# Chunk 0 of a Mamba block between two feed-forward halves: B is turned behind the step-size matmuls

## What is computed

```python
x = x + 0.5 * ffn(layernorm(x), ...)
x = x + mamba(layernorm(x), ...)
x = x + 0.5 * ffn(layernorm(x), ...)
```

```python
proj = einsum('blh,oh->bol', x, W_in)          # h and gate, 1024 channels each
h = silu(causal_conv4(h) + conv_b)
ts, Bm, Cm = split(einsum('bil,oi->blo', h, Wx), [128, 144])
ts, Bm, Cm = rms(ts, dt_ln_w), rms(Bm, b_ln_w), rms(Cm, c_ln_w)
delta = softplus(einsum('blr,ir->bil', ts, Wdt) + dt_bias)
# over l: s = exp(delta * A) * s + delta * B * h ; y = sum_n s * C
y = (y + D * h) * silu(gate)
return einsum('bil,hi->blh', y, Wout)
```

## Time and profile before

| | |
|---|---|
| median of 3 runs | 2776.47 us (2773.37 to 2778.87) |
| the profiled execution | 2791.37 us |
| its span, first to last instruction | 2789.4 us |
| mean granted TensorE clock | 0.912 |
| busy share: TensorE, VectorE, ScalarE, GpSimd | 85%, 88%, 63%, 81% |

### The profile page before, as it was taken

How to read it: one execution, slowest core, us unless ns; L and a number is a source line. 1 busy time by engine, 2 the same in 40 slices (tenths; PEclk the granted TensorE clock), 3 DMA queues, 4 the chain that set the end, 5 groups by cost and what they waited for, 6 DMA issues and landing times. The chain is left out here.

```text
span 2789.4 us, 38187 instructions
## 1 busy us (share of the span) xinstructions
PE 2381.1 (85%) x12266; PEld 1961.2 (70%) x12266; DVE 2461.4 (88%) x3119; ACT 1758.2 (63%) x2995; POOL 2272.8 (81%) x1393
## 2 busy tenths in 40 slices
PE   7888887888688998889988998789987984699968
PEld 6766776676467886677767887677866863577747
DVE  5679997897899998999989999999999987999972
ACT  5585677575657665675568765666667756474531
POOL 2369689789977999699987989699996999888842
PEclk9898998899789999999989999999998996599979
DMA  8754835837575577846787578856788486366634
GB/s 289 261 196 150 299 114 174 303 118 270 175 251 198 165 243 263 295 148 224 235 294 246 157 231 281 304 166 190 237 264 280 122 307 242 106 219 203 231 95 137
DMA packets 293424, 605.61 MB, mean 217 GB/s; under 512 B 23008, under 2 KB 23776, under 8 KB 293216
## 3 DMA queue, kind: packets, MB, share of 16 engines
q1 hardware_dynamic: 293216, 603.08, 64.7%
HBM read 450.42 MB, written 152.57 MB: 216 GB/s over the span
## 5 line engine op out<-in xcount | busy, mean ns | idle before, releaser
L2053 POOL TENSOR_TENSOR sbuf<-dus,bring 128x1024 f32<-128x1024 f32 x512 | 1219.8, 2396 | 175.1 <-PE pt L1489 86.1
L1658 ACT ACTIVATE pa<-dls,cst 128x512 f32<-128x512 f32 x1024 | 699.2, 690 | 498.1 <-DVE sbuf L1840 484.7
L1489 PE MATMUL pt<-ident,sbuf 128*128 128x128 f32 x4096 | 660.7, 298 | 188.3 <-DVE sbuf L1840 68.9
L1489 PEld LDWEIGHTS pt<-ident,sbuf 128*128 128x128 f32 x4096 | 537.3, 154 | 318.2 <-DVE sbuf L1840 98.2
L1407 PE MATMUL pm<-xT,wring 128*128 128x512 f32 x2816 | 712.4, 401 | 17.7 <-DVE xT L1712 9.8
L1840 DVE TENSOR_TENSOR_SCAN sbuf<-pa,carry,sbuf 128x512 f32<-128x512 f32 x512 | 635.7, 1268 | 23.4 <-ACT pa L1658 13.6
L1840 DVE TENSOR_TENSOR_SCAN sbuf<-pa,sbuf 128x512 f32<-128x512 f32 x512 | 605.9, 1207 | 34.3 <-POOL sbuf L2053 19.8
L1851 DVE SCALAR_TENSOR_TENSOR acc<-pt,cT,acc 128x512 f32<-128x512 f32 x768 | 547.5, 737 | 81.3 <-PE pt L1489 71.9
L1420 PE MATMUL pm<-wring,act 128*128 128x512 f32 x2176 | 582.4, 410 | 26.9 <-DMA wring<-wsp 8.0
L1407 PEld LDWEIGHTS pm<-xT,wring 128*128 128x128 f32 x2816 | 519.2, 190 | 120.8 <-issue 17.2
L1420 PEld LDWEIGHTS pm<-wring,act 128*128 128x128 f32 x2176 | 401.7, 193 | 114.2 <-issue 12.0
(11 more groups left out here) (153 smaller groups left out, 2283.8 us busy)
## 6 DMA issues: line engine op xcount, KB each, us to landing
wring<-wsp SPq DMA_DIRECT2D x408, 512.0 KB, 4.3
bring<-b_d SPq DMA_DIRECT2D x256, 256.0 KB, 3.9
xn_d<-tb SPq DMA_DIRECT2D x24, 1024.0 KB, 9.7
xnb<-xn_d SPq DMA_DIRECT2D x19, 1024.0 KB, 7.8
x_d<-tb SPq DMA_DIRECT2D x16, 1024.0 KB, 5.3
sg_d<-hd SPq DMA_DIRECT2D x64, 256.0 KB, 4.5
tb<-x_d SPq DMA_DIRECT2D x16, 1024.0 KB, 7.2
spw<-u_d SPq DMA_DIRECT2D x30, 512.0 KB, 4.5
```

What stands on the lines that cost most here:

```text
L1489: ins = e.matmul(pt[u.pt[tt]][:, k * P:(k + 1) * P], sbuf[:, u.s3, k, tt * P:(tt + 1) * P], ident[:, :], is_transpose=True, start=True, st ...
L1658: e.activation(pa[k % 2][:, :], dls[:, k, :], ACT.Exp, scale=col(C_A + (4 * u.ig + k) * N + u.n)).then_inc(S.a_exp, 1)
L2053: e.tensor_tensor(sbuf[:, u.s3, h * m:(h + 1) * m, :], dus[:, h * m:(h + 1) * m, :], bring[:, u.s2:u.s2 + 1, :].broadcast_to([P, m, TC]), ...
```

## The change

The turn of B leaves the `dt0` unit and becomes a unit of its own, `turn_b`, with the same wait, transposition, copy and stores. For chunks 1 to 7 it is added right behind the turn of ts, as before. For chunk 0 it is added inside `softplus`, behind the `dt` units of the first two quarters and ahead of the softplus steps. So on TensorE and in ScalarE's main thread B's turn and its copy come behind the twelve step-size matmuls and the four copies of their banks. Banks are taken in that order too.

```diff
@@ dt0 @@
         u = self.add("m", Unit("dt0", c))
-        u.ts, u.bn = x.ts, x.bn
+        u.ts = x.ts
@@
         self.bank_free[u.bank] = self.tsT[c] = (u.hi, u.lo)
-        u.bank2, u.bank2_before = self.bank()
-        u.pe2 = self.up(S.p_bt)
-        self.free["bn"] = (u.pe2,)
-        u.bt_before = self.get("bT")
+        if c:
+            self.turn_b(c, x.bn)
+            self.softplus(c, 0)
+        else:
+            self.softplus(c, 0, 1)
+
+    def turn_b(self, c, bn):
+        S = self.S
+        u = self.add("m", Unit("turn_b", c))
+        u.bn = bn
+        u.bank, u.bank_before = self.bank()
+        u.pe = self.up(S.p_bt)
+        self.free["bn"] = (u.pe,)
+        u.before = self.get("bT")
         u.bt = self.up(S.a_bt)
-        self.bank_free[u.bank2] = (u.bt,)
+        self.bank_free[u.bank] = (u.bt,)
         u.kept = self.b_there[c] = self.up(S.st_b, 64)
         self.add("b_out", u)
         self.free["bT"] = (u.kept,)
-        if c:
-            self.softplus(c, 0)
-        else:
-            self.softplus(c, 0, 1)
 
     def softplus(self, c, *parts):
         made = [self.soft_start(c, part) for part in parts]
+        if c == 0 and 0 in parts:
+            self.turn_b(c, self.x_small[c].bn)
         for step in ("soft1", "soft2", "soft3"):
@@ pe_main @@
-                        q.wait_ge(u.bn, *u.bank2_before)
-                        e.matmul(pm[u.bank2][:, 0:P], bn[:, :, :].rearrange("p a b -> p (a b)"), ident[:, :],
+                    elif u.kind == "turn_b":
+                        q.wait_ge(u.bn, *u.bank_before)
+                        e.matmul(pm[u.bank][:, 0:P], bn[:, :, :].rearrange("p a b -> p (a b)"), ident[:, :],
                                  is_transpose=True, start=True, stop=True).then_inc(S.p_bt, 1)
@@ act_main @@
-                        q.wait_ge(u.pe2, *u.bt_before)
-                        e.activation(bT[:, :], pm[u.bank2][:, 0:P], ACT.Copy).then_inc(S.a_bt, 1)
+                    elif u.kind == "turn_b":
+                        q.wait_ge(u.pe, *u.before)
+                        e.activation(bT[:, :], pm[u.bank][:, 0:P], ACT.Copy).then_inc(S.a_bt, 1)
```

## The result

| | before | changed |
|---|---|---|
| median | 2774.92 us (2770.57 to 2778.87, 4 runs) | 2823.05 us (2818.83 to 2827.68, 4 runs) |
| the profiled execution | 2791.37 us | 2827.68 us |
| its span | 2789.4 us | 2825.7 us |
| mean granted TensorE clock | 0.912 | 0.908 |

The ratio is 1.0153, with a 95% interval of 1.0130 to 1.0176. Forecast were 2776.2 us and a range of 2767 to 2785. The profiled execution of before is slower than each of its four runs in this comparison, so the two spans show only 36 of the 48 us. The ratio is worth 42 us (36 to 49), and in the later comparisons the median of before, of 18 to 22 executions each, is 2780.88 to 2785.69 us. So the loss is nearer to 42 than to 48 us.

The account below looks back on a forecast made before the run. VectorE was taken as the bound from 158.64 us on; -0.5 us at Abs and +0.25 us for B's copy gave -0.25 us, so 2776.2 us, with a range of 2767 to 2785 us set by the planned order.

Parts of the forecast that it names:

- What bounds the kernel; B has slack and the step sizes none: VectorE bounds from 158.64 us; in chunk 0 B lands 9.9 us before its product, while step sizes have no slack.
- The wait for bn goes, -0.65 us: Chunk 0's step-size matmuls on TensorE no longer wait for bn and start at 143.85 instead of 144.50 us.
- The clock takes back a part; Abs 0.5 us earlier, the sum -0.25: TensorE's low clock trims the 0.65 us to 0.5 at Abs; with B's copy, VectorE starts 0.25 us earlier.
- the prediction's own sign of being wrong: At chunk 0's step-size matmuls, a low TensorE clock ending later than 147.3 us would show the forecast wrong.
- B's copy between Exp and the adding of one, at 150.3 to 150.9, +0.25 us: In chunk 0 B's copy falls within ScalarE's unbroken work and costs 0.25 us, bounds 0 and 0.28.
- SyncE's queue: Chunk 0's B stores and fetches move later, a gate's store behind them by about 0.8 us; costs nothing.
- Banks, GpSimd's queue: Around chunk 0, five units share five PSUM banks in another order and no GpSimd step moves; no cost.
- The planned order: up to 1.2 us a round, 8.4 us in all: In the seven later rounds, re-planned order shifts each by up to 1.2 us either way, 8.4 if all one sign.
- slower by order: Rival: flipped choices leave VectorE idle longer in each of seven rounds, 8.4 us, giving 2784.6 us; chance 0.18.
- The chances: For the whole kernel: forecast 0.56, B late 0.04, no start gained 0.04, slower and faster by order 0.18 each.
- Within 0.2%: Whole time changes by less than 5.6 us, counted as "same"; chance 0.64.

Follow-up runs that it names:

- e1: Changed kernel's units, waits and banks, with engine lists planned from the kernel before: 2776.73 us, ratio 0.9989 to before.
- e4: Kernel before with one planner constant altered, the margin after another engine's signal, 0.119 instead of 0.12 us: 2793.36 us, ratio 1.0045.
- e5: Changed kernel's units; its own lists up to the planner's 400 us, then what is left of the lists of before: ratio 1.0014.
- e6: Changed kernel's units; its own lists up to the planner's 1000 us, then what is left of the lists of before: ratio 1.0072.
- e7: Changed kernel's units; its own lists up to the planner's 1600 us, then what is left of the lists of before: ratio 1.0090.
- e8: Changed kernel's units; its own lists up to the planner's 2200 us, then what is left of the lists of before: ratio 1.0181.
- e2: Units and banks of the kernel before, with engine lists planned from the changed kernel: 2823.68 us, ratio 1.0143 to before.

## Why the prediction was wrong

- *What bounds the kernel; B has slack and the step sizes none.* Right for chunk 0. B's fetches were issued at 154.19 and the product started at 162.70, behind the same split weight piece as before.
- *The wait for bn goes, -0.65 us.* Right in kind. The next late thing was tsT's low half, done at 144.75 in the changed run; the matmuls followed after 0.27 us, not 0.08. How much the wait had been worth varies: `bn` came 0.47 us behind the low half in before, 0.13 in the changed run (144.88) and ahead of it in e1 (142.49 against 142.55).
- *The clock takes back a part; Abs 0.5 us earlier, the sum -0.25.* The clock's part was mis-sized, with either sign; the rest can be read where the clock is equal. e4 has the units and, up to here, the lists of before, and like the changed kernel it ran this stretch at a clock of 1.00:

```profile
142.66 0.68 DVE L1754 TENSOR_TENSOR tsT<-pm,tsT 128x512 fp32r<-128x512 f32 x1
147.04 1.05 ACT L1607 ACTIVATE spe<-spx 128x1024 f32<-128x1024 f32 x1
156.95 1.22 DVE L1800 TENSOR_TENSOR spe<-spe,spw 128x1024 f32<-128x1024 f32 x1 [0.90 <-ACT spe L1623]
```

  From the low half to Abs it is 3.70 us in e4 and 3.18 in the changed kernel, and to VectorE's first difference 13.61 and 13.12. So Abs gains 0.52 us, as forecast, and the whole -0.49 against the forecast -0.25. (The prediction's 2.8/12 for a full-speed matmul is 0.23 and not 0.24 us, which changes nothing.) The clock itself is worth more: the same program takes 14.87 us in before (158.64 - 143.77) and 13.61 in e4, and e1, with the low clock throughout and Abs behind the fourth copy, 15.85. There the low clock lasts from before 142.8 until past 148.0, the prediction's own sign of being wrong. The rows are of e1 and then of the changed kernel; the last figure but two is the clock:

```profile
142.80:148.00 5.20, 5.19 (x12) 4.00 (x13) 0.00 (x0) 2.06 (x3) 0.00 (x0) 0.50 0.71 283
```

```profile
145.40:147.90 2.50, 2.50 (x14) 2.01 (x12) 0.00 (x0) 1.92 (x3) 0.00 (x0) 1.00 1.05 421
```

- *B's copy between Exp and the adding of one, at 150.3 to 150.9, +0.25 us.* The place is right, the price too high. It started at 150.40 and took 0.28 us. From the start of Exp to that of the adding of one it is 1.11 us with the copy between them and 1.09 without it in e4 (148.55 and 149.64), so the copy fell into a gap there and cost 0.02 us, at the lower bound.
- *SyncE's queue.* The fetches were there by 154.66 + 4.8 = 159.5 at the latest, as forecast. The gate's store went ahead of them, not behind: the new list has it at 153.80.
- *Banks, GpSimd's queue.* Nothing to see, as forecast; e1 holds all of it and isn't slower. The working was wrong, though: `bank()` goes round four banks (`NM = 6 - NT`), neither six nor five. B's turn now waits for the copy of the first step-size bank, which is done near 146.7, before the turn is due at 147.8.
- *The planned order: up to 1.2 us a round, 8.4 us in all.* **This is the step that failed**: the loss is 42 to 48 us, five to six times that price. I had the mechanism, as the rival "slower by order", with its direction, and took its size from the likeness of four rounds of one plan. Cut at the copies of B in the same way, the changed kernel's four rounds are:

```profile
960.20:1284.90 324.70, 289.18 (x1521) 237.36 (x1519) 296.88 (x378) 213.60 (x363) 281.97 (x174) 0.95 0.70 231
1284.90:1618.90 334.00, 295.18 (x1545) 245.14 (x1545) 304.95 (x380) 219.68 (x379) 288.56 (x172) 0.93 0.68 227
1618.90:1945.60 326.70, 289.80 (x1525) 239.11 (x1525) 294.01 (x376) 210.68 (x358) 281.88 (x174) 0.95 0.70 230
1945.60:2249.30 303.70, 271.50 (x1453) 225.80 (x1453) 278.53 (x343) 204.47 (x352) 265.64 (x156) 0.97 0.71 240
```

  They should have been 324, 312, 325 and 311 us within 1.2. VectorE's idle time in them is 27.8, 29.1, 32.7 and 25.2 us, where before it is 22.6, 22.4, 21.3 and 24.8: up to 11.4 us more in a round, and more in each. Within the changed kernel the two odd rounds differ by 30 us in length. So the likeness was a property of the list of before and says nothing of other lists. Even in the earlier trace rows it was less than it seemed, since the odd rounds don't hold equal work: their idle times differ by 2.4 us. By equal work the new list loses 11, 14, 15 and 7 us in successive pieces, all with one sign. The size was to be had ahead of the run: the kernel's own planner puts its new list 40.5 us behind the old one.
- *The chances.* "Within 0.2%" got 0.64 because the direct effect was near zero. With a planner that makes all lists anew from every edit, the direct effect says little about the outcome: e2 and e4 move the time by 1.4% and 0.45% with no unit changed. "Slower by order" had 0.18, and even where it held, its price of 8.4 us kept the range too narrow.

## What to carry to other kernels

Where a list of instructions is made by a planner from estimated times, an edit is two changes: what it does, and a new order of everything behind it. Measure them apart, by running the new instructions with the old list and the reverse, before a gain or a loss is put down to the edit; and see that the old list still means the same instructions. For a forecast, ask the planner for its own end with the new book first, and take the range from what small shifts of its constants do, not from how alike the rounds of one plan are. Here it foresaw the losses and not the gain. A loss that comes from the order alone can be taken back by another order of the same instructions, here by 0.01 us in one constant.

## What was not expected of the hardware

The granted clock over the twelve step-size matmuls differs between executions of the same instructions after nearly the same idle time. The changed kernel, e5, e6, e7 and e8 have the same units, and lists that are the same up to the planner's 400 us. The matmuls took 2.98, 2.99, 2.97, 4.57 and 4.39 us in them, after 2.71, 2.70, 2.69, 2.83 and 2.38 us of idle time; the mean clock from 143.85 to 148.20 in e7 was 0.61. From the low half to VectorE's first difference that is 13.12, 13.12 and 13.10 us against 14.61 and 14.52. So the program alone doesn't set this level, and at this place it outweighs the edit's 0.49 us.

```profile
143.03 2.99 PE L1494 MATMUL pm<-tsT,wdts 128*128 128x512 f32 x12 [2.70 <-DVE tsT L1783]
143.85 4.57 PE L1494 MATMUL pm<-tsT,wdts 128*128 128x512 f32 x12 [2.83 <-DVE tsT L1783]
```

The rows are of e5 and of e7. And two profiled executions with the same lists, before and e1, have spans of 2789.4 and 2764.5 us at mean clocks of 0.912 and 0.921: a single trace is uncertain by more than most edits here are worth.
